# Seven key blocks instead of eight for GpSimd, in half of the attention chunks

## The reference

```python
x = _layernorm(x + _L0_gnn_ref(x, adj, ...))   # normalised adjacency times (x W^T + b)
x = _layernorm(x + _L1_gnn_ref(x, adj, adj, Wq, Wk, Wv, Wo))
x = _layernorm(x + _L2_gnn_ref(x, adj, ...))   # like layer 0, with relu
x = _layernorm(x + _L3_gnn_ref(x, adj, ...))   # graph attention with exp of a leaky relu
```

```python
q = (x @ Wq.T).reshape(d, n, h)          # d = 128 batches, n = 3327, h = 8; k and v likewise
a = jnp.einsum('dnh,dmh->dnm', q, k) * scale
a = a + spatial_encoding + edge_encoding # both are adj
a = jax.nn.softmax(a, axis=2)
out = jnp.einsum('dnm,dmh->dnh', a, v)
```

## Time and profile before

| | us |
|---|---|
| median of 3 runs | 11505.47 (11487.87 to 11508.58) |
| profiled execution | 11497.9 |
| its span | 11496.1 |
| busy in the span: PE / DVE / ACT / POOL | 10376.2 / 9955.6 / 10348.3 / 8142.1 |

### The profile page before, as it was taken

One profiled execution on the slowest core, in us unless ns is written; L12 is line 12 of the kernel. 1 busy time (PEld: TensorE's weight loads), 2 busy tenths in 40 slices (PEclk: granted clock), 3 DMA queues, 4 the chain that ended last, 5 costly groups with the idle time before them and its releaser, 6 DMA issues. The chain is left out here.

```text
span 11496.1 us, 371057 instructions
## 1 busy us (share of the span) xinstructions
PE 10376.2 (90%) x138570; PEld 5332.6 (46%) x138570; DVE 9955.6 (87%) x10280; ACT 10348.3 (90%) x8546; POOL 8142.1 (71%) x4114
## 2 busy tenths in 40 slices
PE   4749999999999999999799999999999999999877
PEld 4614555555445555554344444444444444444473
DVE  7348999999989999999799999999899999999738
ACT  3149999999999999999899999999999999999705
POOL 0007888888878888888688888888788888888500
PEclk7979999999999999999899999999999999999988
DMA  8694444444444444443533333333433333333344
GB/s 327 223 255 66 62 62 62 62 61 61 79 76 61 61 61 61 62 62 56 93 54 55 55 54 54 54 54 55 92 55 55 55 55 55 54 55 54 67 173 161
DMA packets 505792, 943.18 MB, mean 82 GB/s; under 512 B 100727, under 2 KB 453374, under 8 KB 454686
## 3 DMA queue, kind: packets, MB, share of 16 engines
q1 hardware_dynamic: 505724, 942.28, 42.3%
HBM read 799.88 MB, written 142.00 MB: 82 GB/s over the span
## 5 line engine op out<-in xcount | busy, mean ns | idle before, releaser
L1058 DVE SCALAR_TENSOR_TENSOR a_probs<-ps,a_adj 128x768 f32<-128x768 f32 (+1 forms) x9216 | 8973.6, 1019 | 781.5 <-PE ps L948 661.7
L1033 POOL TENSOR_TENSOR a_pool_probs<-a_pool_probs,a_adj 128x768 f32<-128x768 f32 (+1 forms) x4096 | 8125.6, 1984 | 1862.1 <-ACT a_pool_probs L1008 1862.1
L1013 ACT ACTIVATE a_probs<-a_probs 128x1536 f32<-128x1536 f32 (+3 forms) x4096 | 8212.0, 2005 | 14.1 <-DVE a_probs L1058 13.8
L948 PE MATMUL ps<-a_q,a_k 34*128 34x384 f32 (+1 forms) x26624 | 4455.3, 406 | 654.4 <-ACT a_pool_probs L1008 369.5
L1008 ACT ACTIVATE a_pool_probs<-ps 128x768 f32<-128x768 f32 (+1 forms) x4096 | 4491.8, 1097 | 33.2 <-PE ps L948 33.1
L968 PE MATMUL ps<-a_probs,a_v 128*9 128x192 f32 (+1 forms) x73728 | 4011.4, 340 | 0.0
L948 PEld LDWEIGHTS ps<-a_q,a_k 34*128 34x128 f32 x26624 | 2176.8, 185 | 3186.7 <-ACT a_pool_probs L1008 1191.3
L968 PEld LDWEIGHTS ps<-a_probs,a_v 128*9 128x9 f32 x73728 | 1944.6, 91 | 1278.2 <-issue 123.6
L968 PE MATMUL ps<-a_pool_probs,a_v 128*9 128x192 f32 (+1 forms) x32768 | 2217.5, 342 | 2.2 <-POOL a_pool_probs L1033 2.2
L968 PEld LDWEIGHTS ps<-a_pool_probs,a_v 128*9 128x9 f32 x32768 | 486.9, 88 | 987.7 <-issue 981.7
L127 ACT ACTIVATE g_rstd<-g_stat 128x26 f32<-128x26 f32 x2 | 0.5, 225 | 433.3 <-DVE g_stat L118 433.3
(11 more groups left out here) (181 smaller groups left out, 2070.0 us busy)
## 6 DMA issues: line engine op xcount, KB each, us to landing
a_k<-k_parts SPq DMA_DIRECT2D x2048, 208.0 KB
a_v<-v_ext SPq DMA_DIRECT2D x512, 117.0 KB, 3.4
adj_t<-tr SPq DMA_DIRECT2D x26, 1664.0 KB, 6.4
g0tile<-adj_t SPq DMA_DIRECT2D x26, 1664.0 KB, 6.8
g2tile<-adj_t SPq DMA_DIRECT2D x26, 1664.0 KB, 7.0
nat<-in_adj SPq DMA_DIRECT2D x25, 1663.5 KB, 9.9
e_nat<-in_adj SPq DMA_DIRECT2D x25, 1663.5 KB, 6.9
a_q<-q_parts SPq DMA_DIRECT2D x2048, 12.0 KB
```

What stands on the lines that cost most here:

```text
L948: ins = nc.tensor.matmul(ps[:, place + bank:place + bank + half], k_tile[b][row:row + SCORE_ROWS, P * j:P * (j + 1)].bitcast(F32R), q_tile ...
L1013: nc.scalar.activation(sums, sums, ACT.Exp, scale=2.0).then_inc(sums_exped, 1)
L1033: nc.gpsimd.tensor_tensor(flat(k), flat(k), adj_c[:, j, :], ALU.mult).then_inc(multiplied, 1)
L1058: v.scalar_tensor_tensor(out=halves(flat(k)), in0=score(j), scalar=SCALE / 2, in1=halves(adj_c[:, j, :]), op0=ALU.mult, op1=ALU.add).then_ ...
```

## The change

A class `Plan` holds, for each size of chunk, the GpSimd blocks, the sets, the ring slot of each set and of each GpSimd block over two batches, and how far ahead VectorE's scores are written. The chunks of six keep what they had. In the chunks of seven:

- GpSimd has seven blocks (0, 4, 8, 11, 15, 19, 22), VectorE nineteen, in seven sets: five of three blocks and two of two.
- the ring of sets has five slots, given by a list; four are for three blocks, one for two.
- VectorE's scores are written five blocks ahead instead of four.
- since 19 is odd, the two places for scores in PSUM go on alternating from batch to batch (`score_place` now takes k, which tells the batch of the pair).

```diff
-POOL_BLOCKS = (0, 3, 6, 9, 13, 16, 19, 22)
-SETS = ((1, 2), (4, 5), (7, 8), (10, 11, 12), (14, 15), (17, 18), (20, 21), (23, 24, 25))
-RING = 4
+class Plan:
+    def __init__(self, pool_blocks, sets, set_slots, pool_slots, dve_ahead):
+        self.pool_blocks, self.sets, self.set_slots, self.pool_slots = pool_blocks, sets, set_slots, pool_slots
+        self.dve_ahead = dve_ahead
+PLANS = {
+    6: Plan((0, 3, 6, 9, 13, 16, 19, 22),
+            ((1, 2), (4, 5), (7, 8), (10, 11, 12), (14, 15), (17, 18), (20, 21), (23, 24, 25)),
+            (0, 1, 2, 3) * 4, (0, 1, 2, 3) * 4, 4),
+    7: Plan((0, 4, 8, 11, 15, 19, 22),
+            ((1, 2, 3), (5, 6, 7), (9, 10), (12, 13, 14), (16, 17, 18), (20, 21), (23, 24, 25)),
+            (0, 1, 4, 2, 3, 0, 1, 2, 3, 4, 0, 1, 2, 3), (0, 1, 2, 3, 0, 1, 2, 3, 0, 1, 2, 0, 1, 2), 5),
+}
...
-def attention_phase(nc, keep, group, pool_blocks, adj_t, k_parts, q_parts, q_shift, v_ext, o_rows):
+def attention_phase(nc, keep, group, bounded, adj_t, k_parts, q_parts, q_shift, v_ext, o_rows):
...
+    plan = PLANS[nb]
+    pool_blocks = plan.pool_blocks if bounded else ()
...
-        sets, ring, pool_slots = SETS, RING, 4
-        dve_ahead, pool_ahead, set_lag, pool_lag = 4, 1, 5, 7
+        sets, set_slots, pool_slots = plan.sets, plan.set_slots, plan.pool_slots
+        dve_ahead, pool_ahead, set_lag, pool_lag = plan.dve_ahead, 1, 5, 7
...
-        def score_place(j):
-            return 2 * BANK * (DVE_SLOTS if by_pool[j] else dve_rank[j] % DVE_SLOTS)
+        def score_place(k):
+            b, j = k // BLOCKS % 2, k % BLOCKS
+            return 2 * BANK * (DVE_SLOTS if by_pool[j] else (b * n_dve + dve_rank[j]) % DVE_SLOTS)
...
-            return (b * n_sets + set_of[j]) % ring
+            return set_slots[b * n_sets + set_of[j]]
...
-            return pool_ring[(b * n_pool + pool_rank[j]) % pool_slots] if by_pool[j] else \
+            return pool_ring[pool_slots[b * n_pool + pool_rank[j]]] if by_pool[j] else \
```

More of the change, by code:

```diff
@@ L780, in attention_phase @@
     if n_pool:
-        sets, ring, pool_slots = SETS, RING, 4
-        dve_ahead, pool_ahead, set_lag, pool_lag = 4, 1, 5, 7
+        sets, set_slots, pool_slots = plan.sets, plan.set_slots, plan.pool_slots
+        dve_ahead, pool_ahead, set_lag, pool_lag = plan.dve_ahead, 1, 5, 7
     else:
-        sets, ring, pool_slots = [(j, j + 1) for j in range(0, BLOCKS, 2)], 2, 0
+        sets, set_slots, pool_slots = [(j, j + 1) for j in range(0, BLOCKS, 2)], (0, 1) * (BLOCKS // 2), ()
         dve_ahead, pool_ahead, set_lag, pool_lag = 2, 0, 0, 0
@@ L788, in attention_phase @@
     set_of = {j: n for n, js in enumerate(sets) for j in js}
-    set_size = [max(len(js) for js in sets[n::ring]) for n in range(ring)]
+    set_size = [max(len(sets[n % n_sets]) for n, at in enumerate(set_slots) if at == slot)
+                for slot in range(max(set_slots) + 1)]
     def weighed_at(k):
@@ L814, in attention_phase @@
         v_tile = [mem.sb(f"{name}v{b}", [P, BLOCKS, VG]) for b in range(2)]
-        dve_ring = [mem.sb(f"{name}probs{n}", [P, set_size[n], nb, P]) for n in range(ring)]
-        pool_ring = [mem.sb(f"{name}pool_probs{b}", [P, nb, P]) for b in range(pool_slots)]
+        dve_ring = [mem.sb(f"{name}probs{n}", [P, set_size[n], nb, P]) for n in range(len(set_size))]
+        pool_ring = [mem.sb(f"{name}pool_probs{b}", [P, nb, P]) for b in range(len(set(pool_slots)))]
         o_tile = [mem.sb(f"{name}o{b}", [P, acc_cols]) for b in range(2)]
@@ L827, in attention_phase, with score @@
         acc = [ps[:, BANK * (6 + b):BANK * (6 + b) + acc_cols] for b in range(2)]
-        def score_place(j):
-            return 2 * BANK * (DVE_SLOTS if by_pool[j] else dve_rank[j] % DVE_SLOTS)
-        def score(j):
-            return ps[:, score_place(j):score_place(j) + 2 * BANK].rearrange("p (b c) -> p b c", b=2)[:, :, 0:half]
+        def score_place(k):
+            b, j = k // BLOCKS % 2, k % BLOCKS
+            return 2 * BANK * (DVE_SLOTS if by_pool[j] else (b * n_dve + dve_rank[j]) % DVE_SLOTS)
+        def score(k):
+            return ps[:, score_place(k):score_place(k) + 2 * BANK].rearrange("p (b c) -> p b c", b=2)[:, :, 0:half]
         def halves(flat):
@@ L945, in scores @@
                     pe.wait_ge(added, (batch + of) * n_dve + (dve_rank[j] + 1 - DVE_SLOTS))
-                place = score_place(j)
+                place = score_place(k)
                 for row, bank, _ in tiles:
@@ L1007, in turn @@
                         act.wait_ge(scores_ready[True], batch * n_pool + (pool_rank[j] + 1))
-                        nc.scalar.activation(halves(flat(k)), score(j), ACT.Exp,
+                        nc.scalar.activation(halves(flat(k)), score(k), ACT.Exp,
                                              scale=SCALE).then_inc(scores_exped, 1)
@@ L1058, in _ @@
                             v.scalar_tensor_tensor(
-                                out=halves(flat(k)), in0=score(j), scalar=SCALE / 2, in1=halves(adj_c[:, j, :]),
+                                out=halves(flat(k)), in0=score(k), scalar=SCALE / 2, in1=halves(adj_c[:, j, :]),
                                 op0=ALU.mult, op1=ALU.add
@@ L1395, in program @@
             for group in reversed(CHUNK_GROUPS):
-                attention_phase(nc, keep, group, (), adj_t, k_parts, q_parts, q_shift, v_ext, o_rows)
+                attention_phase(nc, keep, group, False, adj_t, k_parts, q_parts, q_shift, v_ext, o_rows)
         with nc.Else():
             for group in reversed(CHUNK_GROUPS):
-                attention_phase(nc, keep, group, POOL_BLOCKS, adj_t, k_parts, q_parts, q_shift, v_ext, o_rows)
+                attention_phase(nc, keep, group, True, adj_t, k_parts, q_parts, q_shift, v_ext, o_rows)
         output_phase(nc, keep, wo, o_rows)
```

## The result

The changed kernel takes 11526.02 us (median of 10 runs, 11510.88 to 11528.89) against 11500.61 for the kernel before on the same chip: ratio 1.0021, 95% interval 1.0012 to 1.0031. It is slower, by about 24 us. The forecast was 11625, with a range of 11550 to 11720: the direction was right, the size five times too large, and the time lies outside the range.

What follows compares the result with a forecast made beforehand. ScalarE sets the pace at 20.63 us a batch; after the change the VectorE and PE loop does at 21.12, so +0.49 x 256 = +125 us. With the median's 7.6 offset, 11625 us, range 11550 to 11720.

Steps and rivals of the forecast that it cites:

- Its part of the change: ScalarE, chunks of seven: one GpSimd exp fewer, seven sets for eight; -0.08 us a batch, alone -21 us in all.
- GpSimd's multiplication worth nothing: GpSimd, chunks of seven: one multiplication of 2.12 us fewer a batch, worth nothing because nobody waits for it.
- The price of a segment: VectorE and PE loop: three additions on, across a triple's weighing, take 3.31 us, against 3.02 for VectorE alone.
- the four exposed places: Additions 14 to 18, 21 to 25, 25 to 3 and 10 to 14: a triple's weighing delays VectorE, 3.31 us each.
- The pairs at 2.06: Additions 18 to 21 and 3 to 6: the score before the weighing is not late, so 2.06 us each.
- The copy's cover against the unfinished weighing: The accumulator's copy must await the weighing of (23-25), which ends 0.1 to 0.2 us before addition 9 ends.
- the step of 1.74 across it: VectorE's step from one addition to the next across the accumulator's copy, 1.74 us against 1.01 for a plain step.
- The fifth triple: Weighing of (23-25) between the scores of blocks 9 and 10: hidden by the copy with 0.4 us to spare.
- (a): Rival, chunks of seven: ScalarE keeps the pace, batches of 20.55 us, -21 us, 11477 us; chance 0.12.
- (b): Rival: ScalarE's lateness delays the pairs' scores and the copy meets unfinished weighing; 21.6 to 21.9 us a batch, 11745 to 11820; chance 0.10.
- (c): Rival: score places free sooner than 0.06 us after an addition; 20.7 to 21.0 us a batch, 11515 to 11590; chance 0.09.
- The rule on grouping: Skill rule cited against the change: larger operations pay on a saturated engine, smaller ones where an engine causes bubbles on others.

Runs made afterwards that it cites:

- the split run: The changed kernel, with the first block of each set of three weighed one position earlier, beside the GpSimd block: 11453.57 us, ratio 0.9963 against the kernel before.
- reordering alone: The kernel before, with only the first block of each set of three weighed one position earlier, beside the GpSimd block: 11508.83 us, ratio 1.0002.

## Why the prediction was wrong, step by step

- ScalarE sets the pace before, with nothing in hand: held. Its part of the change was put at 20.55 us a batch; the split run shows 20.48, so its gain is 0.15 rather than 0.08 us. The 2.36 of the earlier trace rows was read at a set whose exp had waited for its last addition; such exps step 2.35 in the median, and 2.34 where they had not waited. With the unhindered 0.795, 1.589 and 2.337 the two sums are 20.57 and 20.43, a gain of 0.14.
- GpSimd's multiplication worth nothing: held. The view of waits names GpSimd before some weight loads of the changed kernel (27.0 us in the 1000 of the chunks of seven), but nothing is late there: the weighing of block 8 starts 0.81 us after the first of three scores (8933.84 to 8934.65), as it does without GpSimd's name in the earlier trace rows (0.80), and block 8's multiplication had ended at 8932.03.
- The price of a segment, 3.31 us from addition to addition for a run of three blocks: held, to 0.01 us. PE's order and the four exposed places: held. The pairs at 2.06: measured 2.06. The copy's cover against the unfinished weighing, 0.1 to 0.2 us: held, the weighing ends at 8925.95 + 1.32 = 8927.27 and the copy starts at 8927.39.
- The copy: this step failed. The forecast took the step of 1.74 across it as VectorE's own. It costs 0.30, and the 1.74 was PE's. The evidence stood in the rows: the addition after the copy in the earlier trace rows carries "0.18 <-PE", and in the earlier trace rows the scores that start at 8944.55 are those of blocks 6, 10 and 11, so that block 10's was written only after the weighing that ends there. VectorE in the same batch:

```profile
8944.69 0.39 DVE L1044 COPY a_o<-ps 128x224 f32<-128x224 f32 x1
8945.26 4.14 DVE L1058 SCALAR_TENSOR_TENSOR a_probs<-ps,a_adj 128x896 f32<-128x896 f32 x4 [0.19 <-PE ps L948]
```

  The copy itself starts only 0.08 us after the end of the weighing of (23,24,25) (8943.29 + 1.32 = 8944.61), which it has to await, and the addition behind it then waits for its score. The trace of before also has a step of 1.75 into block 23, where there is no copy.
- From this followed a second error with the sign turned round. The fifth triple was called hidden by the copy with 0.4 us to spare; the copy is hidden by the fifth triple. The forecast's own figure for that case, addition 10 at 3.36 after addition 6, is what came: 3.35 in the median.
- With 3.36 in place of 3.76 the round is 21.12 - 0.40 = 20.72 us, as measured, and the sum 11497.9 + 256 x (20.72 - 20.63) = 11521. The mis-sized term is 0.40 x 256 = 102 us of the forecast's 125.
- Rivals. (a), ScalarE keeps the pace, was wrong for this order and right for the split one. The Trainium skill's figure of 93 ns for a start that goes (ScalarE: Activation LUTs, section What ACT_TABLE_LOAD costs) gives an estimate of 0.19 us a batch; the split run shows 0.15, nearer to it than my reading of the earlier trace rows. (b) did not happen here; a pair's exposed run did come when the copy moved, by another cause. (c) had the right size, 11515 to 11590, but the wrong cause: the places in PSUM are free 0.06 us after an addition, as assumed, and the copy made the difference.
- The rule on grouping. The Trainium skill (Perfetto Trace Analysis, section Optimizing Scalar/DVE Operations) says that grouping pays on a saturated engine, and it advises breaking up instructions where ScalarE or VectorE is not saturated but causes bubbles elsewhere. The prediction left out that second condition, and ScalarE was saturated before the change. The first half agrees with the split run, where two starts fewer won 0.15 us. The second was not put to the test: no run splits an exp. What helped was to split PE's run of weighing while ScalarE kept a set of three in one exp.
- ScalarE's lateness holds nothing else up: held, PE's matmuls of scores no longer name its exp. The loads: PE's waits for q 32.1 us, as before.

## What to carry to other kernels

A step between two instructions is a price only if the row shows no wait in it: look for the same step at a place without the operation, and for the releaser beside the row, before putting it into a sum. On an engine whose queue is in order, count the length of a run between two handoffs and not only its total; here moving work between engines alone lost 24 us, reordering alone changed nothing, and both together won about 43 us (by the ratio). When ScalarE appears 100% busy, read the starts, since the recorded intervals cover its waits.

## What the runs showed of the hardware that was not expected

An ACTIVATE's duration in the trace says little of its cost. The exp of a GpSimd block, 128 x 896 from PSUM, steps 0.80 us in the kernel before, in the changed one and in the split one where it isn't held up, but its recorded duration is 1.27, 0.92 and 1.81 us. ScalarE's timeline of the split run:

```profile
8904.42 1.81 ACT L1030 ACTIVATE a_pool_probs<-ps 128x896 f32<-128x896 f32 x1
8905.21 3.35 ACT L1035 ACTIVATE a_probs<-a_probs 128x2688 f32<-128x2688 f32 x1
```

The copy of 224 columns from PSUM costs VectorE 0.30 us in a full queue, with a recorded duration of 0.38. What sets the recorded length of an ACTIVATE was not tried.
